# Layer-norm statistics of the last stage taken during the second attention, in groups of four tiles on GpSimd, and GpSimd normalising the tokens

## What is computed

```python
x = x + tanh(g_xattn[0]) * L0_xattn(layernorm(x), ctx, ctx)          # 16 heads of 8
x = x + tanh(g_ffn[0])   * L0_ffn(layernorm(x))                      # gated mixture of 4 experts
x = x + tanh(g_xattn[1]) * L1_xattn(layernorm(x), ctx, ctx, mask)    # the second attention
x = x + tanh(g_ffn[1])   * L1_ffn(layernorm(x))                      # the last stage

def L1_ffn(x):
    h = bit_linear(x, w1)             # x rounded to 8 bits by token, w1 to -1, 0, 1
    h = silu(conv1d_of_3_taps(h))     # along the tokens, each hidden channel by itself
    return bit_linear(h, w2)          # h rounded to 8 bits by token, w2 to -1, 0, 1

def layernorm(x):
    return (x - mean(x)) / sqrt(var(x) + 1e-5)
```

## Time and profile before

| | us |
|---|---|
| median of three runs | 946.1 (946.05 to 946.44) |
| the profiled execution | 948.64 |
| span of its instructions | 946.9 |
| granted clock of TensorE, mean | 0.992 of full |

### The profile page before, as it was taken

How to read it: one execution, slowest core, us unless ns; L and a number is a source line. 1 busy time by engine, 2 the same in 40 slices (tenths; PEclk the granted TensorE clock), 3 DMA queues, 4 the chain that set the end, 5 groups by cost and what they waited for, 6 DMA issues and landing times. The chain is left out here.

```text
span 946.9 us, 32706 instructions
## 1 busy us (share of the span) xinstructions
PE 915.8 (97%) x11654; PEld 738.8 (78%) x11654; DVE 809.3 (85%) x2348; ACT 765.4 (81%) x1675; POOL 665.6 (70%) x1254
## 2 busy tenths in 40 slices
PE   6999999999989999999899999999999999999996
PEld 3888788877879999998786777778777777777774
DVE  6888898899968898899788888888888869999996
ACT  5888888888877777786666887887888889999995
POOL 5787777776535556556978867676775558999883
PEclk9999999999999999999999999999999999999998
DMA  3501011100000000000000000000000003333333
GB/s 115 186 25 47 25 47 40 32 25 14 14 1 2 1 1 2 1 1 2 1 13 13 15 25 13 26 13 26 13 17 11 3 14 76 76 76 75 74 72 81
DMA packets 54272, 31.17 MB, mean 33 GB/s; under 512 B 38368, under 2 KB 46816, under 8 KB 54112
## 3 DMA queue, kind: packets, MB, share of 16 engines
q1 hardware_dynamic: 54112, 29.08, 11.6%
HBM read 16.48 MB, written 4.19 MB: 22 GB/s over the span
## 5 line engine op out<-in xcount | busy, mean ns | idle before, releaser
L995 DVE TENSOR_REDUCE smax<-score 128x16 f32<-128x1024 f32 x128 | 156.7, 1224 | 63.6 <-DVE a_st L990 38.9
L1363 PEld LDWEIGHTS bank<-vb,prob_t 128*64 128x64 f32 x4096 | 130.2, 138 | 49.8 <-issue 41.8
L1004 DVE TENSOR_TENSOR prob<-score,smax 128x512 f32<-128x512 f32 x256 | 164.8, 685 | 0.8
L642 ACT ACTIVATE prob_t<-bank 128x512 f32<-128x512 f32 x256 | 139.1, 595 | 19.8 <-PE bank L1338 6.1
L637 ACT ACTIVATE prob<-prob 128x512 f32<-128x512 f32 x256 | 147.5, 631 | 5.5 <-DVE prob L1004 5.5
L1363 PE MATMUL bank<-vb,prob_t 128*64 128x18 f32 x4096 | 142.5, 212 | 0.2
L1338 PE MATMUL bank<-const,prob 128*128 128x128 f32 x1024 | 133.3, 273 | 0.7 <-DVE x_all L1105 0.7
L1338 PEld LDWEIGHTS bank<-const,prob 128*128 128x128 f32 x1024 | 115.8, 141 | 1.6 <-DVE x_all L1105 1.1
L721 ACT ACTIVATE eb_t<-eb,gwt 128x128 f32<-128x128 f32 x256 | 81.4, 390 | 34.2 <-POOL eb_acc L494 21.5
L648 ACT ACTIVATE o_t<-bank,b_col 128x128 f32<-128x128 f32 x128 | 48.8, 381 | 65.5 <-PE bank L1338 65.2
L428 POOL TENSOR_SCALAR kj<-k_sb,const 128x512 f32<-128x512 f32 x124 | 85.6, 698 | 21.7 <-issue 21.7
(11 more groups left out here) (169 smaller groups left out, 2343.3 us busy)
## 6 DMA issues: line engine op xcount, KB each, us to landing
ctx_t<-in_ctx SPq DMA_DIRECT2D x32, 256.0 KB, 2.6
x_all<-in_x SPq DMA_DIRECT2D x16, 256.0 KB, 3.5
out_x<-x_all SPq DMA_DIRECT2D x64, 64.0 KB, 1.8
ew<-in_ew SPq DMA_DIRECT2D x2, 512.0 KB, 5.9
q2t<-q2b SPq DMA_TRANSPOSE x64, 2.4
f_cw<-in_f_cw SPq DMA_DIRECT2D x1, 768.0 KB, 7.0
w_t<-in_w_attn SPq DMA_DIRECT2D x2, 256.0 KB, 4.7
f_w<-in_f_w SPq DMA_DIRECT2D x2, 256.0 KB, 6.2
```

Of the source, the lines that this page charges most:

```text
L642: act.activation(prob_t[:, 4 * half:4 * half + 4, :].rearrange("p i q -> p (i q)"), bank[(PT, PT2)[half]], ACT.Copy).then_inc(s["p_copied" ...
L995: dve.tensor_reduce(smax[:].rearrange("p (r h) -> p r h", r=RH), sc, AX.X, ALU.max).then_inc(s["smax_done"], 1)
L1004: dve.tensor_tensor(prob[:, par, half * 512:(half + 1) * 512].rearrange("p (r h k) -> p r h k", r=2, k=S), sc[:, g], m.unsqueeze(3).to_bro ...
L1363: last = pe.matmul(bank[OV][q, i * 2 * VW:(i + 1) * 2 * VW], prob_t[:, i, q], vb[:, k // G, v0 + b * NPAIR + i, :, :].rearrange("p h v -> ...
```

## The change

For the last stage's layer-norm: `bn_stats` and `bn_aggr` of tiles 0 to 58 move into VectorE's steps of the second attention (tile t-5 in step t), `bn_stats` before the maxima and `bn_aggr` between L997 and the subtractions. Tiles 59 to 63 follow in steps 2 to 6 of the last stage. GpSimd computes factor and offset of four tiles with four instructions (`ln_group`) instead of three a tile: groups 0 to 12 at the end of the attention's steps 13, 17, ... 61, groups 13 to 15 in steps 2, 4 and 8 of the last stage. `ln_mv` is two halves of a group each; `ln_rs` and `ln_nr` hold all tiles. From tile 6 on GpSimd normalises the tokens too, after `xdq`; ScalarE does it for tiles 0 to 5 only.

```diff
-        ln_mv = sb("ln_mv", [P, 2, 2])
-        ln_ve = sb("ln_ve", [P, 2, 1])
-        ln_rs = sb("ln_rs", [P, 2, 1])
-        ln_nr = sb("ln_nr", [P, 2, 1])
+        ln_mv = sb("ln_mv", [P, 2, G, 2])
+        ln_ve = sb("ln_ve", [P, G])
+        ln_nm = sb("ln_nm", [P, G])
+        ln_rs = sb("ln_rs", [P, T])
+        ln_nr = sb("ln_nr", [P, T])
...
-        def ln_stats(dve, t, par):
+        LN_STEPS = 4
+
+        def ln_stats(dve, t):
             wait(dve, "x_attn", T + t + 1)
             wait(dve, "ln_mv", t - 1)
-            dve.bn_stats(ln_st[:, par, :], x_tile(t)).then_inc(s["ln"], 1)
+            dve.bn_stats(ln_st[:, t % 2, :], x_tile(t)).then_inc(s["ln"], 1)
 
         def ln_mean_ready(dve, t):
-            wait(dve, "ln_ready", LN_STEPS * (t - 1))
+            if t % G == 0:
+                wait(dve, "ln_ready", LN_STEPS * (t // G - 1))
             wait(dve, "ln", t + 1)
 
-        def ln_mean(dve, par):
-            dve.bn_aggr(ln_mv[:, par, :], ln_st[:, par, :]).then_inc(s["ln_mv"], 1)
-        LN_STEPS = 3
-        def ln_rstd(pool, t, par):
...
+        def ln_mean(dve, t):
+            dve.bn_aggr(ln_mv[:, t // G % 2, t % G, :], ln_st[:, t % 2, :]).then_inc(s["ln_mv"], 1)
+
+        def ln_group(pool, g):
+            def stat(out, a, b, op):
+                pool.tensor_tensor(out, a, b, op).then_inc(s["ln_ready"], 1)
+            def all_tiles(c):
+                return const[:, c:c + 1].to_broadcast([P, G])
+            tiles = slice(G * g, G * (g + 1))
+            wait(pool, "ln_mv", G * (g + 1))
+            wait(pool, "ln_ready", LN_STEPS * g)
+            stat(ln_ve[:], ln_mv[:, g % 2, :, 1], all_tiles(C_EPS), ALU.add)
+            stat(ln_nm[:], ln_mv[:, g % 2, :, 0], all_tiles(C_NEG), ALU.mult)
+            wait(pool, "ln_ready", LN_STEPS * g + 2)
+            stat(ln_rs[:, tiles], ln_ve[:], all_tiles(C_POW), ALU.pow)
+            wait(pool, "ln_ready", LN_STEPS * g + 3)
+            stat(ln_nr[:, tiles], ln_nm[:], ln_rs[:, tiles], ALU.mult)
 
         def ln_apply(act, t, par, free, free_at):
-            wait(act, "ln_ready", LN_STEPS * (t + 1))
+            wait(act, "ln_ready", LN_STEPS * (t // G + 1))
...
@@ GpSimd, attention step, at its end
+                    if L == 1 and j == 1 and t >= 13:
+                        ln_group(pool, (t - 13) // G)
@@ GpSimd, ffn step
-                if has(4):
-                    ln_rstd(pool, t + 4, par)
...
+                if t in (2, 4, 8):
+                    ln_group(pool, {2: NG - 3, 4: NG - 2, 8: NG - 1}[t])
+                if t >= 2 and has(4):
+                    wait(pool, "ln_ready", LN_STEPS * ((t + 4) // G + 1))
+                    wait(pool, "q1_done", t + 3)
+                    wait(pool, "xn_ready", t + 4)
+                    pool.tensor_scalar(xn[:, par, :], x_tile(t + 4), ln_rs[:, t + 4:t + 5], ln_nr[:, t + 4:t + 5],
+                                       ALU.mult, ALU.add).then_inc(s["xn_ready"], 1)
-            lead_in(ffn, -4, -3)
@@ ScalarE, ffn step
-                if has(4):
-                    ln_apply(act, t + 4, par, "q1_done", t + 3)
@@ VectorE, attention step, before the maxima
+                    if L == 1 and has(-5):
+                        ln_stats(dve, t - 5)
@@ VectorE, attention step, between bn_aggr (L997) and the subtractions
+                    if L == 1 and has(-5):
+                        ln_mean_ready(dve, t - 5)
+                        ln_mean(dve, t - 5)
@@ VectorE, ffn step
-                if has(5):
-                    ln_stats(dve, t + 5, o)
+                late = T - 7 + t if 2 <= t < 7 else None
+                if late is not None:
+                    ln_stats(dve, late)
...
-                if has(5):
-                    ln_mean_ready(dve, t + 5)
+                if late is not None:
+                    ln_mean_ready(dve, late)
...
-                if has(5):
-                    ln_mean(dve, o)
+                if late is not None:
+                    ln_mean(dve, late)
@@ VectorE, order of the second attention
-                T - 7: lambda: lead_in(ffn, -5, -5), T - 6: lambda: lead_in(ffn, -4, -4),
```

More of the change, by code:

```diff
@@ L273, in ln_apply @@
         def ln_apply(act, t, par, free, free_at):
-            wait(act, "ln_ready", LN_STEPS * (t + 1))
+            wait(act, "ln_ready", LN_STEPS * (t // G + 1))
             wait(act, free, free_at)
-            act.activation(xn[:, par, :], x_tile(t), ACT.Identity, bias=ln_nr[:, par, :],
-                           scale=ln_rs[:, par, :]).then_inc(s["xn_ready"], 1)
+            act.activation(xn[:, par, :], x_tile(t), ACT.Identity, bias=ln_nr[:, t:t + 1],
+                           scale=ln_rs[:, t:t + 1]).then_inc(s["xn_ready"], 1)
```

## The result

The changed kernel takes 983.99 us (median of 5 runs, 981.07 to 986.11) against 946.05 us before: ratio 1.0397, 95% interval 1.038 to 1.0415. It is slower by 37.9 us. The forecast was 966.8 us with a range of 957 to 975: the right sign, and 17 us short.

A forecast was written before the change was run, and what follows sets the result against it. TensorE's list was taken to bound most second-attention steps, and its wait for GpSimd's L616 the last stage. 26.2 + 0.7 - 0.4 - 7.8 - 0.7 + 2.7 = +20.7 on 946.1 gave 966.8 us, range 957 to 973, to 975 with B.

The forecast's parts named there:

- Part 3: Second attention, steps 13, 17, ... 57: VectorE's mean waits for GpSimd's read of an earlier group, 12 times, +26.2 us.
- Parts 1, 2 and 4: Second attention: added `bn_stats` costs 0, added `bn_aggr` +0.7 and -0.4 us, GpSimd's added group statistics cost 0.
- +0.7: Second attention: the second `bn_aggr` lengthens the fourth step of a group by 0.06 us, in 12 of them.
- -0.4: Three steps before the attention's last: L997 is gone, `bn_aggr` takes its free place, 0.12 us less each.
- Parts 5 and 6: Last stage: other engines' lists fall below TensorE's step, -7.8 and -0.7 us; three grouped statistics on GpSimd, +2.7 us.
- -7.8: Last stage: TensorE sets the step at 2.54 us instead of 2.677 over 57 steps, 7.8 us gained.
- -0.7: Start of the last stage: the first transposes no longer stand behind the per-tile statistics, 0.7 us gained.
- +2.7: Last stage, steps 2, 4 and 8: groups of statistics on GpSimd before the normalisation cost 0.9 us each.
- rival C: Second attention: TensorE's clock falls after each of 12 stalls, 1.7 us lost each time, 987 us; chance 0.03.
- Rivals A and B: A: attention, statistics ready in time, no stall, 940.6 us. B: last stage gains nothing, 974.6 us. Chance 0.08 each.

The follow-up runs named there:

- e1: The changed kernel, but `ln_mv` has room for four groups instead of two and VectorE's mean waits for the read of group g-4; 940.22 us.
- e3: The changed kernel, but GpSimd reads a group at the end of attention step 4g+11 instead of 4g+13, still two halves of `ln_mv`; 939.39 us.
- e6: The kernel before, but GpSimd normalises the tokens from tile 6 on; the statistics stay per tile in the last stage; 964.97 us.
- e5: The kernel of e3, but ScalarE keeps the normalisation of the last stage, so only the statistics have moved; 939.18 us.
- e2: The changed kernel, stall left in, but TensorE does 8 matmuls of 128x128 into a free bank in the 12 stalled steps; 968.24 us.
- e4: The changed kernel, but GpSimd's read in attention step 4g+13 stands before the expansion of k, not behind it and the bias row; 942.71 us.
- e7: The kernel of e3, but tiles 59 to 63 two steps earlier, groups 13 and 14 read around the attention's end, group 15 spread over steps 8 to 11; 938.55 us.
- e9: The kernel of e7, but GpSimd reads group 13 after its first `xdq` (last-stage step -2), not before its lower parts of the tap weights; 937.39 us.
- e8: The kernel of e2, but with 4 instead of 8 matmuls in each of the 12 stalls; 969.06 us.

## Why the prediction was right and wrong

- *Part 3, the wait, +26.2*: right in place, number and size. Twelve waits, steps of 6.25 us where 6.28 was written, 25.8 us. e1 and e3 take it away by room and by place. Its lower bound, 9 us less with four instructions of 0.20 us, should read 11 (12 x 0.93); nothing hung on it.
- *Parts 1, 2 and 4*: right that they are nearly free. The second `bn_aggr` does not even lengthen the fourth step of a group: the +0.7 is a gain of about 0.6 (3.82 us instead of 3.87), whose cause stays open. The 0.12 us was read from another place; between maxima and subtraction the second one moves the subtraction from 1.26 to 1.30 us after the maxima. The -0.4 did not come: the three steps are 3.93, 3.93 and 3.80 us, before 3.93, 3.93 and 3.81.
- *Parts 5 and 6, -7.8, -0.7, +2.7*: right, steps of 2.54 us and 0.9 us a group, -5.7 in all against -5.8. The normalisation on GpSimd takes 0.45 us with two operands by row, not the 0.378 of L616 or the 0.54 of a factor two. The prediction left open which engine held the 2.68 us: by e6 it was GpSimd's list of about 2.6 us with its wait for VectorE's mean, and by e5 not ScalarE.
- *The sum, where it failed*: the step that failed is the one that priced a stall of TensorE by its length alone and put the fall of the clock aside as rival C, with a chance of 0.03 and "the rest of each group is solid work" as the reason. The pause is enough. It was followed by the lower clock in 8 of 12 groups and cost 16.9 us, and e2 shows that it is the clock. The terms as measured are 25.8 + 16.9 - 0.6 - 5.7 = 36.4 us in the profiled execution, the fastest of five; the medians differ by 37.9, and where the other 1.5 us lie was not seen. The price written for C, 1.7 us at each of 12 pauses and 987 us in all, came near 984 partly by luck: five falls cost 1.55 to 1.58 us, three about 3.0, and four pauses had none.
- Rivals A and B did not happen. The Trainium skill (TensorE: Matmul & The Clock Gate, section HAM oscillation), which the prediction cited for C, describes a loop that waits about 3 to 5 us for DMA at every turn and pays for the clock's return each time. The trace agrees that the price comes again and again, 1.55 us or about twice that at each fall; but here the pauses were 2.1 us and 4 of 12 cost nothing.

## What to carry to other kernels

When statistics, copies or any small product pass from one engine to another in groups through two halves of a buffer, write down for each half in which step it is filled again and in which it is read, and where in its own list the reader stands: two steps made 45 us of difference here. A pause of TensorE that recurs can have two prices, its length and the clock afterwards; the second was two thirds of the first here (16.9 and 25.8 us), and where the pause stayed, matmuls that nobody needs were cheaper than idleness (e2). The place in the reader's list counts as much: in front of the expansion that waits for k the read cost 3 us (e4 against e3), behind it 45. And a read that must itself wait belongs behind the work whose place in time matters (e7 and e9).

## What was not expected of the hardware

- A pause of 2.1 us in otherwise full work was followed by a fall of TensorE's clock in 8 of 12 cases, one of 1.1 us (e8) in 3 of 12, one of 0.2 us (e2 and e4) in none of 23; these are counts of one execution each. Each fall cost 1.55 to 1.58 us or about twice that, 3.0 to 3.1, and nothing in between. The five runs of the changed kernel differ by 5 us, more than those of any kernel whose clock stays, and the slowest has the lowest mean clock (0.971, the fastest 0.976). What decides whether a given pause is followed by a fall was not tried.
- A 128x1 instruction with a power on GpSimd takes 0.55 us and its group of four columns 1.02 us, more than a 128x128 `tensor_scalar` at 0.37 to 0.45 us. For such small work the kind and number of instructions count for more than the elements.
- An instruction of VectorE on two columns took 0.90 us instead of 0.16 while GpSimd subtracted 128x512 elements, and ended with the first of these subtractions (e7). In the kernel before, the same instruction (L1307 at 746.52) took 0.23 us beside the end of the same work (742.98 to 746.73).
